# Two transformer layers on one core: where the contexts of three batches and the output biases are made

## The chip, the cores and the metric

The kernel runs on one core of a Trainium2 chip. The metric is the time on the device in microseconds (us). TensorE (PE) does matmuls, and transposes by a matmul with the identity; VectorE (DVE), ScalarE (ACT) and GpSimd (POOL) do the rest; SyncE (SP) issues most DMAs. POOL cannot read PSUM, the memory of eight banks into which TensorE writes.

## The reference

x has 4 batches of 512 rows of 256 values, 2048 rows in all (16 tiles of 128, four a batch). Two layers follow one another; each has a self-attention, a cross-attention and a feed-forward part, each with a residual and a layer norm. What matters here is layer 1:

```
x = layernorm(x + attn(x) @ Wo + bo)                 16 heads of 16, causal, rotary
x = layernorm(x + cross_attn(x, ctx_512) @ Wo + bo)   16 heads of 16, 1601 keys
x = layernorm(x + tree_ffn(x))
```

`attn` is softmax(q k / 4) v for every head. The values' bias is left out of the heads: since a softmax's weights add to one, it adds `bv @ Wo` to the output, so each attention's output bias is `bo + bv @ Wo`, computed on the chip.

## The kernel before

The kernel is a row of programs (`nc.Block`), one after another; in each, every engine has its own list of instructions in a fixed, written order, and waits on semaphores. A program ends when all engines have ended theirs. Around the change stand four:

1. `combine_and_prepare` (line 1504) adds the experts' rows to x, normalizes (the helper class `Tail`), transposes x, and projects queries, keys and values of layer 1's self-attention. VectorE begins with `val.init` (a memset), then for each chunk c of two tiles: `dve_sum`, the gathered rows' addition, `dve_stats`, and `dve_apply` of the chunk before. TensorE: `pe_proj(c)`, `pe_out(c-2)`, projections.
2. `heads_loop` with `causal` (line 1828), the first head loop: 16 groups of four heads of one batch, R = 5 buffers. Each group has four key tiles (kt) with three turns each, so 12 "points": scores of heads 0 and 1, scores of heads 2 and 3 (L2069), values (L2085) of the tile before. ScalarE takes the exponential (L2145), POOL sets the upper triangle to zero (L1981, `triangle`), and ScalarE copies a group's result to `OT` (L2135). Between the points TensorE makes "units" (L2045) for later groups, whose row maxima VectorE takes (L2191); the last group's units are made during group 13, and its shift (L2212, `shift`) is cast early in group 14. PSUM: banks 0 to 3 scores, 4 to 6 units, 7 values.
3. `heads_tail` (line 2238), the tail between the loops. It begins with the biases: VectorE spreads `bv` over columns (L2349), TensorE multiplies (L2293), VectorE adds (L2352). Then per chunk c: TensorE transposes two tiles of OT to rows by query (`by_query`, L2279); VectorE divides by the softmax's sums (`context`: L2343 reciprocal, L2345 product); TensorE turns the context (`pe_in`, L139), ScalarE copies it (L155), TensorE projects it (`pe_proj`, L166), VectorE adds x (`dve_sum`, L193) and takes statistics (L201 to L207), POOL computes rstd (L212), VectorE applies it (`dve_apply`, L219), TensorE transposes the new x (`pe_out`, L139), ScalarE copies it to xT (L256). POOL adds the output bias to x ahead of the sum (`pool_residual`, L132), and sets rows of ones in the key buffers (`ones_tile`, L1728), for which the key loads wait on SyncE. After each of the first two batches, the queries of the cross-attention are projected (L1764), split into bf16 parts (L321, L345, L325, L358) and stored (L368).
4. `heads_loop` without `causal`, the loop of the cross-attention, begins at line 2270's barrier.

VectorE's order in a step of the tail is: contexts of chunk c, apply(c-2), sum(c-1), statistics(c-1), split. TensorE's: `by_query` of chunk c, query blocks, out(c-3), projection(c-1), turn(c).

## Time and profile before

| what | us |
|---|---|
| time, median of 3 runs (lowest, highest) | 1487.79 (1482.65, 1488.82) |
| profiled execution, its own time | 1489.09 |
| its span | 1487.1 |
| the tail's window, from VectorE's first (L2349) to the next loop's first matmul (L2045) | 795.38 to 844.73 |

Line numbers (L193) are those of the kernel before. An instruction's line can be that of a helper, so L139 is both the turn of a context and the transpose of x: the names (psum<-cf_sb,t_cx or psum<-cf_sb,x_sb) tell them apart. "[0.90 <-PE psum L166]" is idle time just before the first instruction of a row and what ended it; "PEq" stands for TensorE's sequencer. PEld is the row of weight loads, which lie beside matmuls. The granted clock is a share of TensorE's 2.4 GHz: 1.00 or 0.50, with means between them.

### The profile page before, as it was taken

How to read it: one execution, taken by the hardware profiler on the slowest of the kernel's cores; microseconds unless marked ns; L12 is line 12 of the kernel's file. 1: busy time of each engine (PE TensorE's matmuls, PEld its weight loads, DVE VectorE, ACT ScalarE, POOL GpSimd, SP SyncE). 2: the span in 40 equal slices, each digit the busy share in tenths (PEclk: the TensorE clock that was granted, in tenths of full speed). 3: DMA queues.
4: the chain of work that ended last, by engine and by line, in shares of the span. 5: the costliest groups of instructions: out<-in, count | busy, mean ns of one | idle time of the engine just before them, and what ended most of it. 6: DMA issues, size and time to landing. Idle time of an engine off the chain costs nothing. (4 is left out here: it accounts for less than half of the span.)

```text
span 1487.1 us, 24888 instructions
## 1 busy us (share of the span) xinstructions
PE 1369.3 (92%) x9358; PEld 762.8 (51%) x9358; DVE 1059.4 (71%) x2351; ACT 774.8 (52%) x1067; POOL 321.7 (22%) x407
## 2 busy tenths in 40 slices
PE   6898899989999989869998889999999999999996
PEld 3565578756899886423335422333333333333285
DVE  4887466662122128968994799999999999997077
ACT  2344266631111112336763316888888888888754
POOL 3110322243000017743335440000000000000011
PEclk9999799999999999969999869999999999999999
DMA  9548533346889842674422650343222343220001
GB/s 341 194 134 246 171 122 128 122 165 226 299 279 302 272 152 79 215 222 143 131 66 60 177 164 2 85 102 80 67 67 68 86 101 80 68 67 2 1 1 57
DMA packets 152841, 198.68 MB, mean 134 GB/s; under 512 B 15723, under 2 KB 124799, under 8 KB 152594
## 3 DMA queue, kind: packets, MB, share of 16 engines
q1 hardware_dynamic: 141004, 165.34, 36.7%
q0 software_dynamic: 9200, 29.64, 6.4%
q10 hardware_dynamic: 2518, 2.13, 0.4%
q8 instruction: 74, 1.21, 0.4%
q14 instruction: 45, 0.37, 0.1%
HBM read 136.08 MB, written 60.70 MB: 132 GB/s over the span
## 5 line engine op out<-in xcount | busy, mean ns | idle before, releaser
L2194 DVE TENSOR_REDUCE xa_part<-psum 128x1 f32<-128x512 f32 (+1 forms) x768 | 462.7, 662 | 20.4 <-PE psum L2045 18.6
L2145 ACT ACTIVATE xa_P<-psum 128x1024 f32<-128x1024 f32 (+1 forms) x416 | 403.4, 1021 | 103.3 <-PE psum L2069 102.6
L2069 PE MATMUL psum<-sa_Q,xa_K 48*128 48x512 bf16 (+3 forms) x1664 | 267.0, 381 | 3.9 <-DMA sa_Q<-xa_mrow 2.9
L2045 PE MATMUL psum<-xa_K,sa_Q 48*128 48x512 bf16 (+1 forms) x768 | 239.3, 388 | 4.4 <-DVE xa_part L2194 1.5
L2085 PE MATMUL psum<-xa_P,xa_V 128*32 128x512 f32 (+1 forms) x1664 | 222.6, 607 | 0.4 <-ACT xa_P L2145 0.4
L2045 PEld LDWEIGHTS psum<-xa_K,sa_Q 48*128 48x128 bf16 x768 | 59.2, 94 | 232.5 <-DVE xa_part L2194 160.8
L2069 PEld LDWEIGHTS psum<-sa_Q,xa_K 48*128 48x128 bf16 (+3 forms) x1664 | 105.6, 97 | 68.7 <-ACT xa_P L2145 20.7
L2191 DVE CUSTOM_DVE_ANT_0 psum<-psum,cf_sb 128x512 f32<-128x512 f32 (+1 forms) x240 | 111.5, 520 | 18.3 <-PE psum L2045 17.5
L1334 PEld LDWEIGHTS psum<-xtT,wgu 128*128 128x128 f32 x992 | 115.5, 192 | 5.8 <-issue 4.6
L1334 PE MATMUL psum<-xtT,wgu 128*128 128x128 f32 x992 | 115.9, 275 | 1.4 <-issue 0.8
L2145 ACT ACTIVATE sa_P<-psum 128x1024 f32<-128x1024 f32 (+3 forms) x128 | 83.4, 702 | 49.1 <-PE psum L2069 49.1
L1483 DVE TENSOR_TENSOR ht<-sgt,psum 128x512 f32<-128x512 f32 x31 | 21.3, 688 | 114.1 <-ACT sgt L1386 114.1
L1386 ACT ACTIVATE sgt<-psum 128x512 f32<-128x512 f32 x31 | 18.5, 597 | 132.6 <-PE psum L1334 132.6
L212 POOL TENSOR_TENSOR t_rstd<-t_ve,mhalf 128x2 f32<-128x2 f32 (+1 forms) x36 | 27.6, 768 | 229.3 <-DVE t_ve L207 229.1
L2045 PE MATMUL psum<-sa_K,sa_Q 48*128 48x512 bf16 (+1 forms) x240 | 64.7, 321 | 12.1 <-PEq L1556 5.5
L2069 PE MATMUL psum<-sa_Q,sa_K 50*128 50x256 bf16 (+7 forms) x512 | 63.9, 308 | 4.0 <-DMA sa_Q<-sa_mrow 2.6
L1994 POOL CAST xa_mh<-xa_mx 128x16 bf16<-128x16 f32 x16 | 3.1, 197 | 293.0 <-DVE xa_mx L2200 266.8
L2085 PEld LDWEIGHTS psum<-xa_P,xa_V 128*32 128x32 f32 (+1 forms) x1664 | 32.9, 108 | 53.5 <-issue 50.6
L634 PE MATMUL psum<-a_in_sb,xT_sb 128*128 128x384 f32 x128 | 48.5, 526 | 12.9 <-DMA xT_sb<-in_xT 10.1
L1215 PE MATMUL psum<-xT_sb,big_weights 128*128 128x512 f32 x128 | 58.8, 614 | 0.7 <-PEq L937 0.7
L1981 POOL TENSOR_SCALAR_AFFINE_SELECT sa_P<-sa_P 128x512 f32<-128x512 f32 x64 | 40.6, 634 | 86.6 <-ACT sa_P L2145 86.6
L1344 PE MATMUL psum<-wdn,ht 128*128 128x256 f32 x248 | 58.7, 380 | 0.6 <-DVE yt L1490 0.6
(250 smaller groups left out, 2140.7 us busy)
## 6 DMA issues: line engine op xcount, KB each, us to landing
wgu<-in_f_gu SPq DMA_DIRECT2D x31, 1024.0 KB, 6.3
xa_K<-kx SPq DMA_DIRECT2D x192, 100.1 KB, 4.9
wdn<-in_f_dn SPq DMA_DIRECT2D x31, 512.0 KB, 6.5
vx<-xv_v SPq DMA_DIRECT2D x48, 256.0 KB, 3.3
xa_V<-vx POOLq DMA_DIRECT2D x16, 768.0 KB, 6.5
sa_Q<-qs SPq DMA_DIRECT2D x64, 96.0 KB, 2.3
sa_K<-ks SPq DMA_DIRECT2D x64, 96.0 KB, 2.3
sa_Q<-qx SPq DMA_DIRECT2D x64, 96.0 KB, 2.3
```

Source lines behind the costliest of these rows:

```text
L212: pool.tensor_tensor(self.rstd[:, u, :], self.ve[:, u, :], self.env.mhalf[:, 0:self.tc], ALU.pow).then_inc(self.s_rstd, 1)
L634: pe.matmul(o, env.xT[:, k, t * P:(t + 1) * P], w["a0_in"][:, k, cols], start=(k == 0), stop=False)
L1215: last = pe.matmul(o, w[name][:, k, f * P:(f + 1) * P], env.xT[:, k, c * L:(c + 1) * L], start=(k == 0), stop=(k == KD - 1))
L1334: last = pe.matmul(GU(j)[:, f * P:(f + 1) * P], wgu[:, u, k, f * P:(f + 1) * P], xtT[:, u, k, :], start=(k == 0), stop=(k == KD - 1))
L1344: last = pe.matmul(Y_PS[:, 0:D], ht[:, u, f, :], wdn[:, u, f, :], start=(f == 0), stop=(f == FC - 1))
L1981: pool.affine_select(square, square, [[0, G], [1, P]], ALU.is_ge, 0.0, base=0, channel_multiplier=-1).then_inc(s_tri, 1)
L2045: last = pe.matmul(out[:, 0:width], hb.q(u)[tile:tile + HALF, to, qt * P:(qt + 1) * P], hb.k(u)[tile:tile + HALF, to, cut[e]:cut[e] + widt ...
L2069: last = pe.matmul(out(j), hb.k(u)[tile:tile + depth, to, kt * P:kt * P + r], hb.q(u)[tile:tile + depth, to, q0(kt):L], start=(half == 0), ...
L2085: last = pe.matmul(O_PS[h * VW:(h + 1) * VW, q0(kt):L], Vg[0:r, u, kt, h * VW:(h + 1) * VW], Pr[0:r, (u * KT + kt) % PR, h, 0:L - q0(kt)], ...
L2145: act.activation(Pr[0:r, (u * KT + kt) % PR, h:h + 2, 0:w_], S_PS(p)[0:r, :, 0:w_], ACT.Exp, scale=SCALE).then_inc(s_exp, 1)
L2191: dve.tensor_tensor_reduce(src[:, 0:k1], src[:, 0:k1], env.later[:, L - k1:L], 1.0, -3e38, ALU.add, ALU.max, mx[:, g % 2, col + qt:col + q ...
L2194: dve.tensor_reduce(part[:, g % 2, col + qt, e:e + 1], src[:, 0:cut[e + 1] - cut[e]], AX, ALU.max).then_inc(s_1free, 1)
```

## The change

The class `OutputBias` takes the bias computation out of the tail and puts it into the combining program: VectorE's two spreading copies ahead of `val.init`, TensorE's eight-matmul product ahead of its first step, VectorE's two additions at the start of step 1, and a wait of TensorE (`pe_free`) before its first projection.

The class `Contexts` holds what makes contexts. During the last 21 points of the first loop (from point 3 of group 14), TensorE makes those of batches 0 to 2, twelve tiles, as `pe_ahead(t)`: `by_query(t)` into banks 4 and 5, and after every second tile the turn of chunk t/2 - 1 into bank 6. VectorE makes the contexts behind its last shift and copies the turned ones into `xT` (no longer needed there), which takes the place of `t3_cT`. At the end of its list in that loop POOL adds the bias to x for chunks 0 and 1. Context and sum buffers lie in columns of `cf` with tables no longer read.

In the tail `pe_proj(0)` comes first. Contexts of tiles 12 to 15 are made in steps 0 and 1, and turned at the head of steps 1 and 2. VectorE's order becomes apply(c-1), sum(c), statistics(c), contexts, split; POOL's residual(c+1), rstd(c), ones, split. `pe_out(c-2)` waits until all turned contexts are copied. The number of steps goes from 11 to 10.

```diff
-        self.r = sb(name + "_r", [P, ring, tc, D], F32)
+        self.r = sb(name + "_r", [P, ring, tc, D], F32) if sums is None else sums
...
+        bias_ = OutputBias(env, c_, sem)
...
@@ -1579,6 +1580,7 @@
             @block.tensor
             def _(pe):
                 pe.sem_inc(tail.s_proj, DONE)
+                bias_.pe_product(pe)
                 for c in range(STEPS):
                     if DONE <= c < CHUNKS:
                         tail.pe_proj(pe, c, lambda k: w["f_wd"][:, k, :],
@@ -1587,6 +1589,8 @@
                         tail.pe_out(pe, c - 2)
                     for n in blocks_at(c):
                         b, name, m = blocks[n]
+                        if n == 0:
+                            bias_.pe_free(pe)
                         if m == 0:
                             pe.wait_ge(tail.s_xT, TB // 2 * (b + 1))
                             item_free(pe, item_of(n))
 
             @block.vector
             def _(dve):
+                bias_.dve_spread(dve)
                 val.init(dve)
                 for c in range(STEPS):
+                    if c == 1:
+                        bias_.dve_add(dve)
                     if c < CHUNKS:
                         u = c % tail.ring
                         tail.dve_sum(dve, c, biased=False)
...
+class OutputBias:
+    def __init__(self, env, c, sem):
+        self.env = env
+        sb, _ = env.alloc(c)
+        self.bvb = sb("bvb", [P, 2, KD, P], F32)
...
+    def ps(self, n):
+        return self.env.PS[:, 7 * BANK + n * D:7 * BANK + (n + 1) * D]
+    def dve_spread(self, dve):
+        for n, of in enumerate("sx"):
+            dve.tensor_copy(self.bvb[:, n, :, :], self.env.w[of + "_bv"].unsqueeze(2).to_broadcast([P, KD, P])).then_inc(self.s_bvb, 1)
+    def pe_product(self, pe):
+        for n, of in enumerate("sx"):
+            pe.wait_ge(self.s_bvb, n + 1)
+            for k in range(KD):
+                last = pe.matmul(self.ps(n), self.bvb[:, n, k, :], self.env.w[of + "_wo"][:, k, :], start=(k == 0), stop=(k == KD - 1))
+            last.then_inc(self.s_bps, 1)
+    def dve_add(self, dve):
+        dve.wait_ge(self.s_bps, 2)
+        for n, of in enumerate("sx"):
+            dve.tensor_tensor(self.env.w[of + "_bo"], self.ps(n), self.env.w[of + "_bo"], ALU.add).then_inc(self.s_bias, 1)
+    def pe_free(self, pe):
+        pe.wait_ge(self.s_bias, 2)
+class Contexts:
+    AHEAD = (B - 1) * TB
+    STEPS = AHEAD + 1
+    def __init__(self, env, c, name, OT):
+        self.env, self.OT = env, OT
+        sb, sem = env.alloc(c)
+        spare = env.cf[:, CF_FIRST:CF].rearrange("p (a u t n) -> p a u t n", a=2, u=2, t=2)
+        self.cx = spare[:, 0]
+        self.tail = Tail(env, c, name, (2, 4, 2), PAIR_TILES, KD, behind=3, inputs=False, sums=spare[:, 1])
+        self.rc = sb(name + "_rc", [P, 2, H], F32)
...
+    def bank(self, t):
+        n = t % 2 + (4 if t < self.AHEAD else 0)
+        return self.env.PS[:, n * BANK:(n + 1) * BANK]
+    def turned(self, c):
+        return self.env.PS[:, 6 * BANK:7 * BANK] if 2 * c < self.AHEAD else self.tail.ps(0, c)
+    def columns(self, c, i, k):
+        return self.env.xT[:, k, (2 * c + i) * P:(2 * c + i + 1) * P]
+    def pe_by_query(self, pe, t):
+        b, i = divmod(t, TB)
+        if t >= 2:
+            pe.wait_ge(self.s_cx, t - 1)
+        for g in range(G):
+            last = pe.transpose(self.bank(t)[:, g * P:(g + 1) * P], self.OT[:, b * G + g, i * P:(i + 1) * P], self.env.ident)
+        last.then_inc(self.s_ops, 1)
+    def pe_in(self, pe, c):
+        if 2 * c < self.AHEAD and c:
+            pe.wait_ge(self.tail.s_cT, c)
+        elif c:
+            pe.wait_ge(self.tail.s_cT, c - 1)
+        pe.wait_ge(self.s_cx, 2 * c + 2)
+        for i in range(2):
+            last = self.tail.turn(pe, self.turned(c), i, self.cx[:, c % 2, i, :])
+        last.then_inc(self.tail.s_cT_ps, 1)
+    def pe_ahead(self, pe, t):
+        if t < self.AHEAD:
+            self.pe_by_query(pe, t)
+        if t >= 2 and t % 2 == 0:
+            self.pe_in(pe, t // 2 - 1)
+    def dve_context(self, dve, t):
+        if t >= 4:
+            dve.wait_ge(self.tail.s_cT_ps, t // 2 - 1)
+        o = self.bank(t).rearrange("p (h n) -> p h n", n=VW)
+        dve.wait_ge(self.s_ops, t + 1)
+        dve.reciprocal(self.rc[:, t % 2, :], o[:, :, HD:HD + 1].rearrange("p h n -> p (h n)")).then_inc(self.s_rc, 1)
+        dve.wait_ge(self.s_rc, t + 1)
+        dve.tensor_tensor(self.cx[:, t // 2 % 2, t % 2, :].rearrange("p (h d) -> p h d", d=HD), o[:, :, 0:HD],
+                          self.rc[:, t % 2, :].unsqueeze(2).to_broadcast([P, H, HD]), ALU.mult).then_inc(self.s_cx, 1)
+    def dve_ahead(self, dve, t):
+        if t < self.AHEAD:
+            self.dve_context(dve, t)
+        if t >= 2 and t % 2 == 0:
+            c = t // 2 - 1
+            dve.wait_ge(self.tail.s_cT_ps, c + 1)
+            dve.tensor_copy(self.env.xT[:, :, 2 * c * P:(2 * c + 2) * P],
+                            self.turned(c).rearrange("p (k n) -> p k n", k=KD)).then_inc(self.tail.s_cT, 1)
...
+    def pe_proj(self, pe, c, w):
+        pe.wait_ge(self.tail.s_cT, c + 1)
+        self.tail.pe_proj(pe, c, w, lambda i, k: self.columns(c, i, k))
...
@@ -1857,6 +1978,13 @@
     assert BEHIND < LEAD and EARLY >= LEAD
+
+    AHEAD_FROM, AHEAD_POINTS = (GROUPS - 2) * POINTS + 3, 20
+
+    def due_ahead(g, point):
+
+        past = g * POINTS + point - AHEAD_FROM
+        return min(contexts.STEPS, past * contexts.STEPS // AHEAD_POINTS + 1) if contexts and past >= 0 else 0
     def due(point, count):
@@ -2017,6 +2145,8 @@
                         triangle(g, kt)
                         if kt == 1 and 1 <= g <= GROUPS - R:
                             reload_v(g - 1, (g - 1) % R)
+                for c in range(2):
+                    contexts.tail.pool_residual(pool, c, lambda t: env.w["s_bo"])
             @block.tensor
             def _(pe):
@@ -2112,6 +2242,10 @@
                                     shift(g + 1)
                             if ahead == 1 and point == LAST_POINT:
                                 shift(g + 1)
+                            for t in range(due_ahead(g, point - 1) if point else due_ahead(g - 1, POINTS - 1), due_ahead(g, point)):
+                                if t == 0:
+                                    pe.wait_ge(s_1free, reduced(shift_at(GROUPS - 1)))
+                                contexts.pe_ahead(pe, t)
                 for n in range(U):
                     if not causal and n in project_at:
@@ -2231,158 +2365,115 @@
                     high(GROUPS - 1)
                     low(GROUPS - 1)
                     shift(GROUPS - 1)
+                    for t in range(contexts.STEPS):
+                        contexts.dve_ahead(dve, t)
                 else:
                     of_cuts(GROUPS - 1)
...
+    tail = contexts.tail
+    LAST = contexts.AHEAD // 2
+    STEPS = CHUNKS + 2
...
             @block.tensor
             def _(pe):
...
                 def query_block(n):
                     if n >= 2:
                         sp_.freed(pe, n - 2)
-                    else:
-                        pe.wait_ge(s_bias, 2)
                     later.project(pe, n, Q_PS(n))
...
                 for c in range(STEPS):
-                    if c < CHUNKS:
-                        for t in PAIR_TILES(c):
-                            by_query(t)
+                    if LAST <= c + LAST - 1 < CHUNKS:
+                        contexts.pe_in(pe, c + LAST - 1)
                     for n in blocks_at(c):
                         query_block(n)
-                    if 3 <= c < CHUNKS + 3:
-                        pe.wait_ge(tail.s_cT, min(c, CHUNKS))
-                        tail.pe_out(pe, c - 3)
-                    if 1 <= c <= CHUNKS:
-                        tail.pe_proj(pe, c - 1, lambda k: wo[:, k, :])
+                    if 2 <= c < CHUNKS + 2:
+                        pe.wait_ge(tail.s_cT, CHUNKS)
+                        tail.pe_out(pe, c - 2)
                     if c < CHUNKS:
-                        tail.pe_in(pe, c, lambda i: cx[:, (2 * c + i) % 4, :], lambda i: pe.wait_ge(s_cx, 2 * c + i + 1))
+                        contexts.pe_proj(pe, c, lambda k: wo[:, k, :])
+                    if c + LAST < CHUNKS:
+                        for t in PAIR_TILES(c + LAST):
+                            contexts.pe_by_query(pe, t)
             @block.scalar
             def _(act):
                 for c in range(STEPS):
+                    if LAST <= c + LAST - 1 < CHUNKS:
+                        contexts.act_in(act, c + LAST - 1)
                     for n in blocks_at(c):
                         sp_.act_hi(act, n, Q_PS(n))
-                    if 3 <= c < CHUNKS + 3:
-                        tail.act_out(act, c - 3)
-                    if c < CHUNKS:
-                        tail.act_in(act, c)
+                    if 2 <= c < CHUNKS + 2:
+                        tail.act_out(act, c - 2)
                     for n in blocks_at(c):
                         sp_.act_mid(act, n)
             @block.gpsimd
             def _(pool):
-                pool.wait_ge(s_bias, 1)
                 for c in range(STEPS):
+                    if 2 <= c + 1 < CHUNKS:
+                        tail.pool_residual(pool, c + 1, lambda t: bo)
                     if c < CHUNKS:
-                        tail.pool_residual(pool, c, lambda t: bo)
-                    if queries and c < 2 * hb.RING:
-                        pool.wait_ge(tail.s_xb, c + 1)
+                        tail.pool_rstd(pool, c)
+                    if c < 2 * hb.RING:
+                        pool.wait_ge(tail.s_rstd, c + 1)
                         hb.ones_tile(pool, c // 2, c % 2).then_inc(s_ones, 1)
                         pool.wait_ge(s_ones, c + 1)
-                    if 1 <= c <= CHUNKS:
-                        tail.pool_rstd(pool, c - 1)
                     for n in blocks_at(c):
                         sp_.pool_lo(pool, n)
             @block.vector
             def _(dve):
...
                 for c in range(STEPS):
+                    if 1 <= c <= CHUNKS:
+                        tail.dve_apply(dve, c - 1)
                     if c < CHUNKS:
-                        for t in PAIR_TILES(c):
-                            context(t)
-                    if 2 <= c < CHUNKS + 2:
-                        tail.dve_apply(dve, c - 2)
-                    if 1 <= c <= CHUNKS:
-                        tail.dve_sum(dve, c - 1)
-                        tail.dve_stats(dve, c - 1)
+                        tail.dve_sum(dve, c)
+                        tail.dve_stats(dve, c)
+                    if c + LAST < CHUNKS:
+                        for t in PAIR_TILES(c + LAST):
+                            contexts.dve_context(dve, t)
                     for n in blocks_at(c):
                         sp_.dve_rest(dve, n, Q_PS(n))
...
@@ -2736,11 +2827,12 @@
         with ExitStack() as c1:
             sb1, _ = alloc(c1)
             OT = sb1("OT", [P, GROUPS, L], F32)
-            heads_loop(nc, env, "sa", sa, OT, keys=later_keys)
+            contexts = Contexts(env, c1, "t3", OT)
+            heads_loop(nc, env, "sa", sa, OT, keys=later_keys, contexts=contexts)
             with ExitStack() as c2:
                 xa = HeadBuffers(env, c2, "xa", CTX, False, stacks(env.qx), kx_part, env.vx, Q=sa.Q)
-                later = heads_tail(nc, env, "t3", OT, "s", "x", xa)
+                later = heads_tail(nc, env, contexts, "s", xa)
                 heads_loop(nc, env, "xa", xa, OT, queries=later)
             l1_out(nc, env, OT, env.w["x_wo"])
```

## Rows read from the trace of the kernel before

**Rows 1.** The page, part 1: busy time, share of the span, instructions.

```profile
PE 1369.3 (92%) x9358; PEld 762.8 (51%) x9358; DVE 1059.4 (71%) x2351; ACT 774.8 (52%) x1067; POOL 321.7 (22%) x407
```

**Rows 2.** Windows, first head loop: busy us of PE, PEld, DVE, ACT, POOL; clock; DMA.

```profile
764.50:772.70 8.20, 7.57 (x82) 3.26 (x81) 7.73 (x37) 5.43 (x10) 2.54 (x4) 1.00 0.02 4
...
781.00:794.00 13.00, 9.96 (x116) 3.05 (x116) 0.00 (x0) 9.34 (x17) 5.08 (x8) 1.00 0.01 2
```

**Rows 3.** Timeline, loop's end: start, duration (us), engine, line, operation, [idle before].

```profile
780.18 0.28 DVE L2212 CAST sa_mrow<-psum 32x128 bf16<-32x128 f32 x1 [0.40 <-PE psum L2054]
...
793.07 0.64 POOL L1981 TENSOR_SCALAR_AFFINE_SELECT sa_P<-sa_P 128x512 f32<-128x512 f32 x1 [0.42 <-ACT sa_P L2145]
...
793.76 0.42 PE L2085 MATMUL psum<-sa_P,sa_V 128*32 128x128 f32 x8 [0.42 <-POOL sa_P L1981]
...
794.25 0.60 ACT L2135 ACTIVATE OT<-psum 128x512 f32<-128x512 f32 x1 [1.25 <-PE psum L2085]
...
795.38 0.29 DVE L2349 COPY t_bvb<-s_bv_sb 128x256 f32<-128x256 f32 x1 [14.92 <-PEq L1917]
```

**Rows 4.** Timeline, the tail's first steps and the next loop's first matmul.

```profile
797.21 1.91 PE L2293 MATMUL psum<-x_wo_sb,t_bvb 128*128 128x256 f32 x4
...
799.16 0.42 DVE L2352 TENSOR_TENSOR s_bo_sb<-psum,s_bo_sb 128x256 f32<-128x256 f32 x1 [3.28 <-PE psum L2293]
...
799.67 1.41 POOL L132 TENSOR_TENSOR x_sb<-x_sb,s_bo_sb 128x256 f32<-128x256 f32 x2 [5.96 <-DVE s_bo_sb L2352]
...
802.43 1.97 PE L166 MATMUL psum<-s_wo_sb,t_cT 128*128 128x256 f32 x8
...
804.56 0.90 PEld L2279 LDWEIGHTS psum<-cf_sb,OT 128*128 128x128 f32 x8
...
844.73 0.96 PE L2045 MATMUL psum<-xa_K,sa_Q 48*128 48x512 bf16 x3 [1.00 <-PEq L2270]
```

**Rows 5.** Timeline, VectorE and POOL in the tail.

```profile
804.44 0.69 DVE L193 TENSOR_TENSOR t_r<-psum,x_sb 128x512 f32<-128x512 f32 x1 [0.90 <-PE psum L166]
...
806.23 0.17 DVE L207 TENSOR_SCALAR t_ve<-t_mv 128x2 f32<-128x2 f32 x1
806.31 0.26 DVE L2343 RECIPROCAL t_rc<-psum 128x16 f32<-128x16 f32 x1
...
808.78 0.68 DVE L193 TENSOR_TENSOR t_r<-psum,x_sb 128x512 f32<-128x512 f32 x1
...
811.90 1.27 DVE L219 TENSOR_SCALAR x_sb<-t_r,t_mv,t_rstd 128x256 f32<-128x256 f32 x2
813.09 0.68 DVE L193 TENSOR_TENSOR t_r<-psum,x_sb 128x512 f32<-128x512 f32 x1
...
823.30 0.69 DVE L193 TENSOR_TENSOR t_r<-psum,x_sb 128x512 f32<-128x512 f32 x1 [1.52 <-PE psum L166]
...
839.50 0.68 DVE L193 TENSOR_TENSOR t_r<-psum,x_sb 128x512 f32<-128x512 f32 x1
...
841.53 0.69 POOL L212 TENSOR_TENSOR t_rstd<-t_ve,mhalf 128x2 f32<-128x2 f32 x1 [0.94 <-DVE t_ve L207]
...
842.26 0.74 DVE L219 TENSOR_SCALAR x_sb<-t_r,t_mv,t_rstd 128x256 f32<-128x256 f32 x2 [0.80 <-POOL t_rstd L212]
```

**Rows 6.** Windows around both boundaries; the clock stands third from the end.

```profile
796.00:800.00 4.00, 4.00 (x15) 3.24 (x15) 0.84 (x3) 0.00 (x0) 0.33 (x1) 0.57 0.01 2
...
848.00:852.00 4.00, 4.00 (x8) 1.11 (x6) 2.51 (x4) 0.69 (x1) 0.00 (x0) 0.50 0.59 159
```

**Rows 7.** Timeline of the combining program's start.

```profile
560.27 5.57 PE L166 MATMUL psum<-big_weights,hT 128*128 128x256 f32 x16 [6.18 <-DVE t_r L193]
...
564.77 0.73 DVE L219 TENSOR_SCALAR x_sb<-t_r,t_mv,t_rstd 128x256 f32<-128x256 f32 x2
565.68 0.60 PE L139 MATMUL psum<-cf_sb,x_sb 128*128 128x128 f32 x4
```

**Rows 8.** Window of the combining program's middle.

```profile
580.00:600.00 20.00, 20.00 (x83) 14.40 (x82) 17.01 (x31) 6.32 (x12) 12.95 (x11) 1.00 0.19 64
```

More of the change, by code:

```diff
@@ L82, with __init__ @@
 class Tail:
-    def __init__(self, env, c, name, banks, tiles, kc, behind=0, inputs=True, copied=False, slots=None, scaled=False):
+    def __init__(self, env, c, name, banks, tiles, kc, behind=0, inputs=True, copied=False, slots=None, scaled=False, sums=None):
         self.env, self.tiles, self.kc, self.banks, self.behind = env, tiles, kc, banks, behind
@@ L2385, in heads_tail, with _, keys @@
-    return later if queries else None
+            @block.sync
+            def _(sp):
+                def keys(g):
+                    sp.wait_ge(s_ones, 2 * g + 2)
+                    hb.load_k(sp, g, g)
+                keys(0)
+                for dst, src in env.loads["d"]:
+                    sp.dma_start(dst, src).then_inc(s_wd, 16)
+                keys(1)
+                for n in range(KD):
+                    sp_.sp_out(sp, n)
+                sp_.sp_end(sp, KD)
+                hb.load_q(sp, 0, 0)
+                for n in range(KD, 2 * KD):
+                    sp_.sp_out(sp, n)
+                sp.wait_ge(s_wd, 16 * len(env.loads["d"]))
@@ L2389, in l1_out @@
+    return later
 def l1_out(nc, env, OT, wo):
```

86 lines of the change are left out of this document (19 added, 67 removed).

## The prediction

> **What bounds the kernel now.** I read part 1 of the page first: TensorE is busy 92% of the span, but that is an average over a dozen stages [rows 1]. The change touches three stretches, so I read each by itself.
>
> The first is the last two groups of the first head loop. The per-window view shows VectorE stop at 780.46 us (its last cast); then it does nothing, while a window of 8.2 us before had it busy for 7.73 [rows 2, 3]. TensorE shows 9.96 us busy in 13, so 3.04 us free [rows 2]. The order is a chain: scores, exponential on ScalarE, triangle on POOL, values. After the last triangle (ends 793.71) come the last values (794.18) and the copy to OT (794.85); then the program ends on all engines together, since VectorE, long done, is released only at 795.38, "<-PEq L1917" [rows 3].
>
> The second is the tail, 795.4 to 844.7. Chunk 0 reaches its sum (L193) at 804.44, chunk 7 at 839.50, and the next loop's first matmul stands at 844.73 [rows 4, 5]. In an ordinary chunk VectorE is the busy one: sum at 804.44, variance at 806.23, two contexts from 806.31 to 807.57, apply, next sum at 808.78, 4.34 us with no idle time. Before the sum at 823.30 it waits 1.52 us for TensorE, which had query projections ahead [rows 5].
>
> The third is the start of the combining program: TensorE busy from 560.27 with `pe_proj`, VectorE's apply from 564.77 to 565.50, and TensorE's transpose behind both at 565.68 [rows 7].
>
> **The change, part by part.**
>
> *Contexts in the loop.* Four transposes for each of twelve tiles and each of six chunks: 72 on TensorE. Eight took 0.90 us of weight-load row, 0.112 each [rows 4], so 8.1 us are added within points 3 of group 14 to 10 of group 15. VectorE's share (12 x 0.64, from two contexts in 1.26 us, and six copies of about the 0.68 us of L193) is 12 us, hidden in its 14 us idle [rows 2, 5]; it cannot start before the cast at 780.46. TensorE is not idle enough: 8.1 - 3.04 = 5.1 us longer if all idle time is filled. Laying the steps into the order by hand (each transpose group behind its scores or values, values behind the triangle, and the last turn behind context 11, 0.5 us) I get 5.6. Bounds: 8.1 if nothing hides; and 0 if the matmuls' ends overstate, since the weight-load row is busy only 3.05 us of the 13 [rows 2]. I take 5.6, nearer to the busy row.
>
> Here the Trainium skill ("Perfetto Trace Analysis", "Identifying the Most-Contended Engine") speaks for the change: it says that matmul busy share is not a good measure of TensorE's closeness to its limit, and asks for the weight-load share instead. By that 77% of the window is free and the growth is near 0; it feeds the second rival below. Against it stands that a group still has its chain of waits.
>
> *Two residuals on POOL at the loop's end.* `pool_residual` of chunks 0 and 1 stands behind the last triangle in POOL's order: four additions, two in 1.41 us [rows 4], so 2.9 us after 793.71. The copy to OT ends 1.14 us after it. As all engines leave together, the end moves by 1.75 us, whatever the growth. In the tail the same additions lay beside other work. Bounds: 0 (if POOL did not have to be waited for) and 2.9.
>
> *The tail's start.* From 794.85 to the first sum now 9.59 us pass: bias copies, products, additions, two tiles' contexts, the turn, the copy, the projection. After: 0.6 us to leave and enter, then `pe_proj(0)` at once. At full clock it takes 1.97 us [rows 4]. But the granted clock was 0.57 in the window 796 to 800, after TensorE had been idle from 794.18 to 795.73, and four 256-column matmuls then took 1.91 us with the last one's end [rows 3, 4, 6]. With POOL's residuals the idle time is 3 us, so I count eight at that pace: 3.6. So 4.2 us instead of 9.59, 5.4 saved; 7.0 at full clock. First sum: 804.44 + 5.6 + 1.75 - 5.4 = 806.4.
>
> *Sum 0 to sum 7, now 35.06 us* [rows 5]. Chunks 2 to 7 lose their contexts; chunks 6 and 7's are made in steps 0 and 1. But TensorE's order in steps 1 and 2 is turn(6), projection(1) and turn(7), transposes out(0), projection(2), and turn(c) waits for contexts that VectorE makes after its statistics. Sum 0 to the end of two contexts is 3.2 us, then turn and projection 2.5: 5.75 instead of 4.34. In step 2 out(0) waits also for ScalarE's copy (`wait_ge(tail.s_cT, CHUNKS)`), so contexts 3.2, turn 0.5, copy 0.7, out 0.5, projection 1.9 and a handover: 7.0 instead of 4.31. That loses 4.1. The five later intervals are 26.4 us now. They lose 6.3 of contexts on VectorE's row, but behind them appears what they hid: statistics to rstd 0.25, rstd 0.69, then apply 0.74, so an undisturbed interval is 1.78 + 0.25 + 0.69 + 0.04 + 0.74 = 3.5 [rows 5]. And four of the five hold query projections (3.6 us of TensorE before the chunk's own), their split on VectorE (1.3) or POOL's residual ahead of rstd. Walked through: 3.8, 4.5, 4.9, 5.6, 4.7 = 23.5, a gain of 2.9. Sum: 36.3, 1.2 longer. Bounds: 35.06 - 6 x 1.26 = 27.5, and 41 (third rival).
>
> Apply depends on what POOL does: 1.27 us for two while POOL added residuals, 0.74 with POOL idle [rows 5]. POOL's memsets of the key rows (1.43) now follow rstd and lie on apply, and no row has that overlap; 0.74 to 1.27 per chunk, and I take 1.2 in the first six.
>
> The Trainium skill ("GPSIMD Engine Reference", "Key points") says that GpSimd shares its SBUF interfaces with VectorE and contends with instructions in a 2-port mode or with two inputs. Apply's rows agree (1.27 against 0.74); whether a memset contends too no row here shows.
>
> *SyncE.* The key loads wait for the memsets, which follow rstd: keys(0) goes out some 5 us later, keys(1) to about 834. Stores of the first queries then queue for a microsecond or two; the query load still lands before the end. I cost it at nothing; with more delay it would be next.
>
> End of tail: 806.4 + 36.3 + 5.2 (sum 7 to the next loop, unchanged) = 847.9 against 844.73: +3.2.
>
> *Biases in the combining program.* VectorE gets two copies ahead of its memset (0.29 each at 0.21 distance, 0.45) and two additions ahead of sum 1 (0.42 each at 0.34 distance, 0.76) [rows 3, 4]. Apply(0) then ends 1.2 later, at 566.7, against TensorE's transpose at 565.68: TensorE, which then has no idle time (20.00 of 20 us) [rows 8], starts 1.0 later. The products themselves lie in its idle time before 560.27 [rows 7]. +1.0; bounds 0 and 1.2. A warmer clock for `pe_proj(2)` (5.57 us, 3.62 is usual) gives nothing, since apply(0) is then last.
>
> Sum: +3.2 + 1.0 = +4.2 us. The profiled run took 1489.09 (span 1487.1), 1.3 over the median 1487.79; I apply the difference to the median: 1492.
>
> **Rivals.**
>
> 1. Forecast: transposes lengthen the loop, POOL's residuals and the order in steps 1 and 2 eat what the shorter start gives. +1 to +7, 1489 to 1495. Chance 0.5.
>
> 2. Faster: VectorE's row decides the tail. Then six chunks lose 1.26 us each: 35.06 to 27.5, the end at 806.4 + 27.5 + 5.2 = 839.1, -5.6, and with +1.0 the time is 1483. If TensorE also hides half the growth (-2.8) 1480. For it: no idle time on VectorE in the ordinary chunks. Against: TensorE's order behind the contexts, and VectorE's wait for TensorE at 823.30 already [rows 5]. It decides if turn(6) and turn(7) cost projection(1) and (2) nothing. Chance 0.25, half of it beyond 0.5%.
>
> 3. Slower: the clock. TensorE idles 3 us at the boundary and then works in pieces; at 848 to 852, four us after the next loop's start, the clock still stood at 0.50 though the row was full [rows 6]. If it stays at 1.2 GHz through step 2, projections 1 and 2 cost 1.6 more each and three groups of transposes 0.45 each: +4.6, 1497; with the loop's transposes unhidden (+2.5) 1499. It decides if the granted clock in the tail's first 12 us is under 0.7. Chance 0.25, nearly all beyond 0.5%.
>
> **Numbers.** A median can tell about 0.5% (7.4 us) from no change: below 1480.4, above 1495.2. Faster 0.13 (half of rival 2), slower 0.25 (rival 3 and the forecast's edge), same 0.62. Range 1481 to 1498: rival 2 without its best end, rival 3 without its worst. The forecast's own range is 1489 to 1495.
>
> **What would show it.** Loop: the last OT copy at about 800.5, triangles no longer followed at once by values. Boundary: POOL's L132 as the last before the barrier, some 1.7 us behind the OT copy. Tail: sum 0 at 806 to 807; intervals of 5.7 and 7 before sums 1 and 2 with VectorE waiting for projection; then 3.8 to 5.6. Combining: every stage from 566 on 1 us later. I am wrong if the loop's end moves by under 2 us, if steps 1 and 2 take 4.3, or if the clock stays down.

## The result, and the profile after

The changed kernel takes 1498.7 us (median; lowest 1494.72), the kernel before 1486.99 beside it: ratio 1.0079, 95% interval 1.0060 to 1.0098. It is slower by 11.7 us; I had forecast 4.2, and 1498 as the upper end. One run of this kernel (3370 us) and one of e10 (1911 us) fell into a slow state: their medians count them (1497.5 and 1495.9 without), their ratios do not. The profiled execution took 1502.37 us (span 1500.4). A second series of the same kernel (e11, below) gave 1.0089 [1.0070, 1.0109], 14.3 us.

Part 1 of the page says little, as before [rows 1]:

```profile
PE 1376.4 (92%) x9358; PEld 767.8 (51%) x9358; DVE 1069.4 (71%) x2357; ACT 770.8 (51%) x1061; POOL 320.9 (21%) x407
```

So I cut both traces at the same events. "Combining" runs from the last copy of the feed-forward part (L1490 after) to the loop's first matmul, "loop's end" from group 13's copy to OT to the last one, "start" from that copy's end to sum 0 (L193).

| stretch, us | before | forecast | after | e11 |
|---|---|---|---|---|
| combining | 99.05 | +1.0 | 101.04 | 101.06 |
| loop up to group 13's copy | 134.74 | 0 | 133.74 | 134.73 |
| loop's end | 13.24 | +5.6 | 19.98 | 19.97 |
| start | 9.59 | -3.65 | 6.36 | 6.52 |
| sum 0 to sum 7 | 35.06 | +1.2 | 42.84 | 41.37 |
| sum 7 to the next loop | 5.23 | 0 | 5.69 | 5.68 |

(The forecast's -3.65 is 1.75 for the residuals less 5.4 for the start.) e11's stretches add up to 12.4 us more than before, 8.3 above the forecast: 5.1 of them in sum 0 to sum 7, 1.1 at the loop's end, 1.0 in combining, 0.6 at the start, 0.5 at the end. The line that failed is sum 0 to sum 7. Its seven intervals, for the kernels that the argument needs:

| us | 1 | 2 | 3 | 4 | 5 | 6 | 7 |
|---|---|---|---|---|---|---|---|
| before | 4.34 | 4.31 | 4.29 | 5.92 | 6.44 | 5.08 | 4.68 |
| forecast | 5.75 | 7.0 | 3.8 | 4.5 | 4.9 | 5.6 | 4.7 |
| after | 7.30 | 9.55 | 5.10 | 5.09 | 5.51 | 5.63 | 4.66 |
| e11, the same kernel | 7.20 | 7.10 | 5.10 | 5.09 | 5.53 | 6.66 | 4.69 |
| e2, residuals in the tail | 5.76 | 9.62 | 5.10 | 5.09 | 5.52 | 5.63 | 4.67 |
| e9, fillers on TensorE | 5.76 | 7.09 | 5.10 | 5.09 | 5.52 | 5.63 | 4.67 |
| e3, memsets moved | 7.25 | 7.11 | 4.30 | 4.24 | 4.24 | 6.25 | 4.68 |
| e5, projection first | 5.13 | 5.10 | 5.08 | 5.09 | 5.51 | 6.70 | 4.68 |
| e8, one batch ahead | 4.65 | 4.31 | 4.31 | 5.76 | 6.98 | 4.78 | 4.68 |

Timeline after, TensorE at the boundary and in steps 1 and 2 (columns as in [rows 3]):

```profile
800.99 0.86 PE L2215 MATMUL psum<-sa_P,sa_V 128*32 128x256 f32 x16
805.57 3.27 PE L166 MATMUL psum<-s_wo_sb,xT_sb 128*128 128x256 f32 x8 [3.72 <-PEq L2045]
808.63 1.45 PE L1868 MATMUL psum<-cf_sb,OT 128*128 128x128 f32 x8
812.24 0.63 PE L139 MATMUL psum<-cf_sb 128*128 128x128 f32 x4 [2.15 <-DVE cf_sb L1894]
812.71 3.44 PE L166 MATMUL psum<-s_wo_sb,xT_sb 128*128 128x256 f32 x8
815.93 1.22 PE L1868 MATMUL psum<-cf_sb,OT 128*128 128x128 f32 x8
819.54 0.94 PE L139 MATMUL psum<-cf_sb 128*128 128x128 f32 x4 [2.38 <-DVE cf_sb L1894]
821.16 1.12 PE L139 MATMUL psum<-cf_sb,x_sb 128*128 128x128 f32 x4 [0.69 <-ACT xT_sb L1908]
822.07 3.62 PE L166 MATMUL psum<-s_wo_sb,xT_sb 128*128 128x256 f32 x8
```

The order in steps 1 and 2 is as forecast: projections 1 and 2 stand behind a turn that waits for VectorE's contexts (2.15, 2.38 us), step 2 also for ScalarE's copy (0.69). Projection 0 takes 3.27 us, near the 3.6 forecast; but projections 1 and 2 take 3.44 and 3.62, where I had counted 1.9. The windows (columns as in [rows 2]) show TensorE in pieces and at a low clock:

```profile
804.00:808.00 4.00, 2.43 (x7) 2.05 (x8) 0.00 (x0) 0.00 (x0) 0.00 (x0) 0.76 0.00 2
808.00:812.00 4.00, 2.09 (x10) 1.57 (x9) 2.95 (x10) 0.00 (x0) 1.01 (x2) 0.82 0.00 0
812.00:816.00 4.00, 3.76 (x13) 3.01 (x14) 2.08 (x3) 0.60 (x1) 2.57 (x3) 0.61 0.00 0
...
820.00:824.00 4.00, 3.31 (x12) 2.56 (x11) 1.37 (x2) 1.25 (x3) 1.87 (x3) 0.50 0.34 85
```

VectorE and POOL after, around sums 1 to 3:

```profile
812.01 2.06 DVE L219 TENSOR_SCALAR x_sb<-cf_sb,t_mv,t_rstd 128x256 f32<-128x256 f32 x2
816.18 0.69 DVE L193 TENSOR_TENSOR cf_sb<-psum,x_sb 128x512 f32<-128x512 f32 x1 [2.10 <-PE psum L166]
...
825.73 0.69 DVE L193 TENSOR_TENSOR cf_sb<-psum,x_sb 128x512 f32<-128x512 f32 x1 [4.37 <-PE psum L166]
...
828.51 2.40 DVE L219 TENSOR_SCALAR x_sb<-cf_sb,t_mv,t_rstd 128x256 f32<-128x256 f32 x2 [0.81 <-POOL t_rstd L212]
830.83 0.68 DVE L193 TENSOR_TENSOR cf_sb<-psum,x_sb 128x512 f32<-128x512 f32 x1
```

```profile
827.78 0.69 POOL L212 TENSOR_TENSOR t_rstd<-t_ve,mhalf 128x2 f32<-128x2 f32 x1 [5.83 <-DVE t_ve L207]
828.53 1.42 POOL L1735 MEMSET xa_K<- 32x1601 f32 x1
830.04 1.46 POOL L132 TENSOR_TENSOR x_sb<-x_sb,s_bo_sb 128x256 f32<-128x256 f32 x2
```

Apply starts at 828.51, the memset at 828.53: 2.40 us for the pair, against 1.27 beside residual additions and 0.74 with POOL idle [rows 5].

### The profile page after: what moved, and what is told of

It is laid out like the page before. It is cut to its first block and busy times, and to the rows that moved or that the text cites. A ratio compares the mean times of both kernels' runs of the same rounds, so it can differ in the third digit from the quotient of the medians.

```text
span 1500.4 us, 24878 instructions
## 1 busy us (share of the span) xinstructions
PE 1376.4 (92%) x9358; PEld 767.8 (51%) x9358; DVE 1069.4 (71%) x2357; ACT 770.8 (51%) x1061; POOL 320.9 (21%) x407
## 5 line engine op out<-in xcount | busy, mean ns | idle before, releaser
L2215 PEld LDWEIGHTS psum<-xa_P,xa_V 128*32 128x32 f32 (+1 forms) x1664 | 33.0, 108 | 53.6 <-issue 50.3
```

The lines of the kernel that those rows point to most:

```text
L2215: last = pe.matmul(O_PS[h * VW:(h + 1) * VW, q0(kt):L], Vg[0:r, u, kt, h * VW:(h + 1) * VW], Pr[0:r, (u * KT + kt) % PR, h, 0:L - q0(kt)], ...
```

## The experiments

All ratios are to the kernel before on the same chip, with 95% intervals. Stages that an edit does not touch differ by 1 to 3 us between two profiles (the rest of the span after the tail was 639.6 to 643.0 us in all), so an edit is judged by its own stretch, and the median says what is left of it. "Tail" is the time from the last copy to OT to the next loop's first matmul: 49.88 us before, 54.89 in the changed kernel's first profile, 53.57 in e11's.

**e1, the bias part alone** (the kernel before, with `OutputBias` and nothing of `Contexts`):

```diff
 (kernel before, heads_tail)
-                dve.wait_ge(s_bps, 2)
-                for n, of in enumerate((here, later_)):
-                    dve.tensor_tensor(w[of + "_bo"], B_PS(n), w[of + "_bo"], ALU.add).then_inc(s_bias, 1)
...
 (combine_and_prepare)
+                    if c == 1:
+                        bias_.dve_add(dve)
```

> The kernel before with the biases alone moved to the combining program; the tail keeps its contexts. Theory (each part has its own price, and the contexts' part carries the loss): the first sum comes some 4 us earlier after the loop's end (9.59 us to about 5.5), the combining program ends about 1.0 us later, so 2 to 4 us faster than before, about 1484. Rival (the biases' move carries part of the loss): the combining program loses 3 us or more and the time is not under before's.

Measured: 1486.55 against 1487.11, ratio 1.0004 [0.9990, 1.0018]. The start went from 9.59 to 6.86 us (I had expected about 5.5), sum 0 to sum 7 stayed at 35.06. Combining grew by 0.36. So the start is 2.7 us shorter in this profile; the 2 to 4 us that I expected in the median are not there.

**e2, the residuals of chunks 0 and 1 back in the tail:**

```diff
 (POOL, end of the first loop)
-                for c in range(2):
-                    contexts.tail.pool_residual(pool, c, lambda t: env.w["s_bo"])
 (POOL, start of the tail)
+                for c in range(2):
+                    tail.pool_residual(pool, c, lambda t: bo)
```

> The changed kernel with POOL's residuals of chunks 0 and 1 taken out of the first loop's list and put at the head of POOL's list in the tail. Theory (they hold the loop's end, and a program that POOL ends last is left 1 us later still): TensorE's first matmul of the tail comes at most 1 us after the last OT copy instead of 3.1, and the time falls by 2 to 3 us from the changed kernel's. Rival (the barrier costs the same whoever is last; only 1.4 us of POOL's work goes): 1.4 us, and 1.6 us still pass from the last instruction to the first.

Measured: 1496.96, ratio 1.0064 [1.0043, 1.0086]; the start fell from 6.36 to 2.31 us. Its timeline, POOL, ScalarE and TensorE:

```profile
801.42 0.64 POOL L2109 TENSOR_SCALAR_AFFINE_SELECT sa_P<-sa_P 128x512 f32<-128x512 f32 x1 [1.80 <-ACT sa_P L2277]
803.72 2.79 POOL L132 TENSOR_TENSOR x_sb<-x_sb,s_bo_sb 128x256 f32<-128x256 f32 x4 [1.67 <-POOLq L2045]
```

```profile
802.83 0.60 ACT L2267 ACTIVATE OT<-psum 128x512 f32<-128x512 f32 x1 [1.47 <-PE psum L2213]
```

```profile
803.73 1.97 PE L166 MATMUL psum<-s_wo_sb,xT_sb 128*128 128x256 f32 x8 [0.97 <-PEq L2045]
```

The next program starts 0.30 us after ScalarE's end (803.43) and 1.67 after POOL's (802.06). In the changed kernel it starts 3.05 after ScalarE's end and again 1.67 after POOL's (801.12 + 2.78 = 803.90; 805.57). So the residuals cost their whole length. Projection 0, after 0.97 us of idle instead of 3.72, ran at full clock here; the short idle time alone does not secure that, since in e6, after the same 0.97, it took 3.63 (below). With projection 1 at full clock too, interval 1 is 5.76; interval 2 is 9.62, as in the first profile, with projection 2 at the low clock.

```profile
801.12 2.78 POOL L132 TENSOR_TENSOR x_sb<-x_sb,s_bo_sb 128x256 f32<-128x256 f32 x4
```

**e3, POOL's memsets away from apply** (three in front of rstd(0), two and one behind the residuals of steps 0 and 1):

```diff
...
+                early = {0: (3, 4), 1: (5,)}
...
+                for n in range(3):
+                    ones(n)
                 for c in range(STEPS):
-                    if 2 <= c + 1 < CHUNKS:
-                        tail.pool_residual(pool, c + 1, lambda t: bo)
                     if c < CHUNKS:
                         tail.pool_rstd(pool, c)
-                    if c < 2 * hb.RING:
-                        pool.wait_ge(tail.s_rstd, c + 1)
-                        hb.ones_tile(pool, c // 2, c % 2).then_inc(s_ones, 1)
-                        pool.wait_ge(s_ones, c + 1)
+                    if 2 <= c + 2 < CHUNKS:
+                        tail.pool_residual(pool, c + 2, lambda t: bo)
+                        if c in early:
+                            pool.wait_ge(tail.s_xb, c + 3)
+                    for n in early.get(c, ()):
+                        ones(n)
```

> The changed kernel with POOL's memsets of the key rows taken from behind rstd: three at the tail's head, two in step 0, one in step 1. Theory (a memset on POOL holds back VectorE's apply, 2.40 us a pair beside it against 0.74 alone): from chunk 2 on apply falls to 0.75 to 1.3 us, and the tail is 4 to 6 us shorter. Rival (apply is slow by the residual addition behind it, or by its new buffer in cf): apply stays at 2 us or more.

Measured: intervals 3 to 5 are 4.30, 4.24, 4.24 instead of 5.10, 5.09, 5.51 (-2.9 us); apply, with a residual beside it:

```profile
828.67 1.54 DVE L219 TENSOR_SCALAR x_sb<-cf_sb,t_mv,t_rstd 128x256 f32<-128x256 f32 x2 [0.88 <-POOL t_rstd L212]
830.14 0.68 DVE L193 TENSOR_TENSOR cf_sb<-psum,x_sb 128x512 f32<-128x512 f32 x1
...
832.91 1.54 DVE L219 TENSOR_SCALAR x_sb<-cf_sb,t_mv,t_rstd 128x256 f32<-128x256 f32 x2 [0.81 <-POOL t_rstd L212]
```

The edit moved the residual too, to a place beside apply, and apply is shorter all the same: the memset is the cause of its 2.40 us. The median, 1497.84, ratio 1.0076 [1.0054, 1.0099], does not show the gain.

**e4 and e9, TensorE kept busy** by matmuls of no use: e4 with twelve behind the loop's last values and eight in steps 0 and 1, e9 with six and three.

```diff
                 values(GROUPS - 1, (GROUPS - 1) % R, KT - 1, None)
+                if contexts:
+                    for n in range(12):
+                        pe.matmul(PS[:, 4 * BANK:4 * BANK + D], env.ident, env.w["s_wo"][:, n % KD, :], start=True, stop=True)
 (tail, behind the transposes of steps 0 and 1)
+                        for n in range(8):
+                            pe.matmul(PS[:, 7 * BANK:7 * BANK + D], env.ident, wo[:, n % KD, :], start=True, stop=True)
```

> The changed kernel with idle matmuls of TensorE whose result nobody reads: 12 behind the last values of the first loop, 8 after the transposes of steps 0 and 1. Theory (the low clock in the tail's first 20 us costs 4 to 5 us): the granted clock stays over 0.9 from 804 to 828, projection 0 to 2 take 1.9 us instead of 3.3 to 3.6, and the sums 0 to 2 come 4 us earlier. Rival (VectorE's contexts and not TensorE's pace set sums 1 and 2): the clock is kept and the sums stay within 1 us of the changed kernel's, or fillers delay the turns and the time grows.

> The changed kernel with TensorE kept busy by fewer fillers than in e4_clock_kept: six 256-column matmuls of no use behind the loop's last values (they took 0.44 us each there, so 2.6 us beside the 3.7 us in which TensorE waits at the boundary), and three behind the transposes of steps 0 and 1. Theory (the low clock costs the first two intervals 2 to 4 us, and e4 gave it back by fillers that stood in the way): projections 1 and 2 at under 2.2 us, sum 0 to sum 7 at 39 to 41 us, tail at 50 to 52 instead of 54.9, median 3 to 5 us under the changed kernel's, 1494 to 1496. Rival (the clock is a companion, the interval is set by the waits for contexts): clock 1.00 but sum 0 to sum 7 still above 41.5, median 1497 to 1500.

Measured, e4: 1499.58, 1.0087 [1.0067, 1.0107]. Each filler took 0.45 us, 3.6 for eight, and they delayed what stood behind them: the start is 7.01, intervals 1 and 2 are 6.49 and 7.84 (tail 53.02), although the projections are back at 1.9. e9: 1498.53, 1.0075 [1.0062, 1.0089]. Its clock is 1.00 in every window of 4 us from 796 to 832, and intervals 1 and 2 are 5.76 and 7.09, where I had worked out 5.75 and 7.0. TensorE in e9's steps 0 to 2:

```profile
807.22 1.97 PE L166 MATMUL psum<-s_wo_sb,xT_sb 128*128 128x256 f32 x8 [0.94 <-PEq L2045]
809.02 1.04 PE L1868 MATMUL psum<-cf_sb,OT 128*128 128x128 f32 x8
809.89 1.46 PE L2421 MATMUL psum<-s_wo_sb,cf_sb 128*128 128x256 f32 x6
812.58 0.63 PE L139 MATMUL psum<-cf_sb 128*128 128x128 f32 x4 [1.23 <-DVE cf_sb L1894]
813.04 1.89 PE L166 MATMUL psum<-s_wo_sb,xT_sb 128*128 128x256 f32 x8
...
820.14 1.89 PE L166 MATMUL psum<-s_wo_sb,xT_sb 128*128 128x256 f32 x8
```

So the excess in those two intervals is the low clock. (e2's interval 1 of 5.76, without fillers, says the same.) The tail is 49.60 us, 5.3 shorter than in the first profile of the changed kernel and 4.0 than in e11's; the median is not lower. I can't place that: in e9's profile the loop up to group 13 took 135.91 and the rest after the tail 642.74 us, 1.2 and 2.8 more than in e11's, and medians can't say which of these is typical.

**e5, projection ahead of the turn in steps 0 to 2:**

```diff
                 for c in range(STEPS):
+                    if c <= 2:
+                        contexts.pe_proj(pe, c, lambda k: wo[:, k, :])
                     if LAST <= c + LAST - 1 < CHUNKS:
                         contexts.pe_in(pe, c + LAST - 1)
...
-                    if c < CHUNKS:
+                    if 2 < c < CHUNKS:
                         contexts.pe_proj(pe, c, lambda k: wo[:, k, :])
```

> The changed kernel with projection(c) ahead of turn(c+5) in TensorE's steps 1 and 2. Theory (projections 1 and 2 are late because they stand behind turns that wait for VectorE's contexts): sum 1 comes 5 us or less after sum 0 (7.3 in the changed kernel) and sum 2 some 5 us after sum 1 (9.55); the tail is 4 to 6 us shorter. Rival (the low clock is what makes them late): TensorE stays at half clock and the tail is at most 2 us shorter.

Measured: 1494.3, ratio 1.0050 [1.0031, 1.0069]; the median is 4.4 us under the changed kernel's, on another chip and with overlapping intervals of the ratio. Intervals 1 and 2 are 5.13 and 5.10, set by VectorE's row, although projection 0 met the low clock (tail 49.81).

```profile
806.83 3.75 PE L166 MATMUL psum<-s_wo_sb,xT_sb 128*128 128x256 f32 x8 [3.71 <-PEq L2045]
810.37 1.73 PE L1868 MATMUL psum<-cf_sb,OT 128*128 128x128 f32 x8
811.94 1.89 PE L166 MATMUL psum<-s_wo_sb,xT_sb 128*128 128x256 f32 x8
813.98 0.64 PE L139 MATMUL psum<-cf_sb 128*128 128x128 f32 x4
```

**e6 and e10, e2, e3 and e5 together**, in e10 also with fillers (four at the loop's end, three in steps 0 and 1, two in steps 2 to 7):

```diff
...
 (e10, TensorE, behind the transposes; e6 has none of it)
+                        for n in range(3):
+                            pe.matmul(PS[:, 7 * BANK:7 * BANK + D], env.ident, wo[:, n % KD, :], start=True, stop=True)
+                    elif c < CHUNKS:
+                        for n in range(2):
+                            pe.matmul(PS[:, 0:D], env.ident, wo[:, n % KD, :], start=True, stop=True)
```

> The changed kernel with the residuals in the tail, the memsets early and the projections first, all three. Theory (each has its own price): from the last OT copy to the next loop's first matmul it takes 42 to 45 us against 54.9 in the changed kernel and 49.9 before, and the time comes to about before's, 1485 to 1489, since the loop's 6.7 us and the combining program's 1 stay. Rival (the repairs share one cause, the clock): 48 us or more, 1493 or more.

> e6_three_repairs with fillers for TensorE: four behind the loop's last values, three in steps 0 and 1, two in each step from 2 to 7. In e6 the clock fell to 0.50 to 0.64 in three stretches, and projections took 3.63 and 3.57 us, a query projection 5.26. Theory (the clock is what ate the three repairs): projections 1.9 us, query projections 3.6, intervals 4.3 to 5, sum 0 to sum 7 at 34 to 36 instead of 39.5, tail at 43 to 46 instead of 49.2, median 1488 to 1490. Rival (the engines' order and VectorE's row hold it, a full clock changes little, and sixteen fillers of 0.2 to 0.4 us cost some of it): tail at 48 to 50, median 1492 to 1495.

Measured, e6: 1493.46, 1.0054 [1.0032, 1.0075], tail 49.19 us, no shorter than with one repair alone (49.4 to 50.3, that is 4.5 to 5.5 from 54.89 and 3.2 to 4.2 from e11's). e10: 1496.38, 1.0060 [1.0045, 1.0074], tail 49.23, with a clock of 1.00 from 796 to 840 but for 0.66 and 0.91 in two windows. So a full clock with fillers in the way does not shorten e6; what it would give without them stays open. What holds e10 back stands in its VectorE row: waits for POOL, where three memsets stood ahead of rstd(0), and for projections, where fillers and query projections stood ahead. e6's row has waits for the same two (1.16, 0.87 and 0.81 for POOL; 1.64, 1.28 and 3.25 for projections), and its first projection met the low clock.

```profile
800.65 3.63 PE L166 MATMUL psum<-s_wo_sb,xT_sb 128*128 128x256 f32 x8 [0.97 <-PEq L2045]
```

(This row is e6's, the next ones are e10's.)

```profile
810.53 1.55 DVE L219 TENSOR_SCALAR x_sb<-cf_sb,t_mv,t_rstd 128x256 f32<-128x256 f32 x2 [2.66 <-POOL t_rstd L212]
...
822.80 0.69 DVE L193 TENSOR_TENSOR cf_sb<-psum,x_sb 128x512 f32<-128x512 f32 x1 [1.12 <-PE psum L166]
...
829.27 0.69 DVE L193 TENSOR_TENSOR cf_sb<-psum,x_sb 128x512 f32<-128x512 f32 x1 [2.14 <-PE psum L166]
```

```profile
805.30 4.39 POOL L1735 MEMSET xa_K<- 32x1601 f32 x3
809.78 0.71 POOL L212 TENSOR_TENSOR t_rstd<-t_ve,mhalf 128x2 f32<-128x2 f32 x1
```

**e7, the loop's 48 transposes to rows by query made twice:**

```diff
-        for g in range(G):
+        for g in range(G) if t >= self.AHEAD else [*range(G)] * 2:
             last = pe.transpose(self.bank(t)[:, g * P:(g + 1) * P], ...
```

> The changed kernel with the 48 transposes of OT in the loop's last groups issued twice, VectorE's and ScalarE's work as it is. Theory (TensorE is full there and every transpose lengthens the loop): from the OT copy of group 13 to the last one it takes 25 to 27 us, against 20.0 in the changed kernel and 13.2 before. Rival (waits for contexts and for VectorE are what lengthens it): 20 to 22 us.

Measured: 1502.92, ratio 1.0117 [1.0087, 1.0146]; the loop's end grew from 19.98 to 24.76, 4.78 / 48 = 0.10 us a transpose. Each further transpose lengthens the loop. TensorE's matmul row is full there, though its weight-load row is not (windows of the changed kernel, then of e7):

```profile
787.00:800.00 13.00, 12.80 (x124) 7.35 (x123) 8.29 (x23) 5.90 (x10) 2.54 (x4) 1.00 0.00 0
```

```profile
787.00:800.00 13.00, 13.00 (x126) 8.93 (x125) 6.56 (x17) 5.23 (x9) 1.90 (x3) 1.00 0.01 1
```

**e8, only one batch's contexts in the loop**, the rest in the tail one chunk after another, with the residuals in the tail, the projection ahead of the turn, POOL's memsets behind the residuals instead of behind rstd, and the bias part kept:

```diff
-    AHEAD = (B - 1) * TB
+    AHEAD = TB
...
 (TensorE's step: turn last)
...
-                        pe.wait_ge(tail.s_cT, CHUNKS)
+                        pe.wait_ge(tail.s_cT, min(c + 1, CHUNKS))
                         tail.pe_out(pe, c - 2)
...
+                    if LAST <= c + LAST - 1 < CHUNKS:
+                        contexts.pe_in(pe, c + LAST - 1)
...
```

> The changed kernel with one batch's contexts (4 tiles) in the loop instead of three, residuals in the tail, contexts of chunk c+2 made in step c with projection first, the memsets between residuals as before. Theory: the loop is only 2 to 2.5 us longer than before's (24 transposes instead of 72), the first sum comes 3 us after the last OT copy instead of 9.6, chunks take 4.3 us: the time is 1482 to 1485, faster than both kernels. Rival (a tail that starts at once only meets the low clock, and its order costs as much): within 2 us of before's.

Measured: 1484.02 against 1487.23, ratio 0.9975 [0.9964, 0.9986]: faster than both kernels, by 0.25% against the one before. The loop's end grows by 1.36 us for 24 transposes, the start is 2.53, sum 0 to sum 7 35.47, the tail 43.67 instead of 49.88 us; combining takes 2.0 of it back. Against e6, which moves three batches with much the same order, the loop's end is 5.4 us shorter and the tail 5.5. VectorE has no idle time in an ordinary chunk: rstd is ready behind the contexts.

```profile
808.81 0.25 DVE L1894 RECIPROCAL t_rc<-psum 128x16 f32<-128x16 f32 x1
809.09 0.43 DVE L1896 TENSOR_TENSOR cf_sb<-psum,t_rc 128x256 f32<-128x256 f32 x1
809.43 1.27 DVE L219 TENSOR_SCALAR x_sb<-cf_sb,t_mv,t_rstd 128x256 f32<-128x256 f32 x2
810.62 0.68 DVE L193 TENSOR_TENSOR cf_sb<-psum,x_sb 128x512 f32<-128x512 f32 x1
```

**e11, the changed kernel again:**

> The changed kernel as it is, for a second profiled execution and more times. The profiled execution of the changed kernel took 1502.4 us, above the kernel's median of 1498.7, and e9's tail was 5.3 us shorter in its profile while its median was the same. If the low clock in steps 1 and 2 is there in every execution: sum 0 to sum 7 again at 42 to 43, tail at 54 to 55, with projections of 3.4 to 3.6 us. If it is a matter of the single execution: projections 1 and 2 partly at 1.9 to 2.2, tail at 50 to 53, and the profiled execution at 1497 to 1500. Either way the median stays at 1497 to 1500, and the loop's growth (the 19.98 us from group 13's copy to the last) and the gap of 1.67 us behind the last residual stay as they were.

Measured: 1499.59 against 1485.29, 1.0089 [1.0070, 1.0109]. Interval 1 is 7.20 again, interval 2 is 7.10 instead of 9.55 (projection 2 at 1.89 us): the 2.45 us in interval 2 are there in some executions (the first, and e2's with 9.62) and not in others (e11, e3, e7: 7.10 or 7.11). In interval 6 e11 lost 1.0 us in which VectorE waited for a projection: the query projection ahead of it took 5.37 us instead of 3.67, in a window with a clock of 0.68.

## Why the prediction was wrong

1. **Sum 0 to sum 7: the step that failed**, forecast +1.2, measured +7.8 (e11: +6.3). The order of TensorE in steps 1 and 2 was read rightly: e9, at full clock, has its two intervals within 0.1 us of the forecast. Two prices were missing. The clock: I took it at full after projection 0, it fell again, and intervals 1 and 2 were 4.1 us longer than worked out (e11: 1.55). I had that as rival 3, with a chance of 0.25 and the same price of 1.6 us a projection; its condition (under 0.7 in the first 12 us) was too strict, the windows show 0.76, 0.82 and 0.61. And the memsets: I took apply beside one at up to 1.27 us, because no row had the overlap; it takes 2.05 to 2.42. Intervals 3 to 7 are 26.0 instead of 23.5; e3, without the overlap, has 23.7 (in sum: its intervals 5 and 6 are 0.7 under and over the forecast). 4.1 + 2.5 is the whole excess of 6.6 in the first profile; e11's 5.1 is 1.55 plus 2.5 plus 1.0 in interval 6, which is the low clock again.

   That 1.27 was no upper bound stood in the trace of before: one pair of applies there took 2.08 us, beside POOL's split (L358). The memsets had harmed nothing, since they lay beside sums: 0.68 us each, as with POOL idle (0.69 at 816.18 after).

```profile
813.08 1.46 POOL L1728 MEMSET xa_K<- 32x1601 f32 x1
...
826.65 2.27 POOL L358 TENSOR_TENSOR xq_parts<-xq_rest,xq_parts 128x512 bf16<-128x512 f32 x2 [0.55 <-ACT xq_parts L325]
827.74 2.08 DVE L219 TENSOR_SCALAR x_sb<-t_r,t_mv,t_rstd 128x256 f32<-128x256 f32 x2
```

   (Rows of the kernel before; the sum beside the memset, at 813.09, is in [rows 5].)

2. **The residuals at the loop's end.** I let the program end with whichever engine ended last and counted 1.75 us. The trace of before already had the distance: the last triangle ends at 793.71 and VectorE is released at 795.38, 1.67 later, while ScalarE's 794.85 [rows 3] is only 0.53 before. With the same 1.67 in the later profiles, POOL decided there too, so a longer POOL moves the start by all of its 2.78. From the OT copy's end to sum 0 I had 5.95 us and it took 6.36: 3.05 to the next program's first matmul where I had 2.35, and 3.31 for the projection where I had 3.6.

3. **The loop's growth**, 5.6 forecast, 6.74 measured, is inside its bounds. Only 8.1 - 6.7 = 1.4 us of transposes found TensorE idle, an estimate at my price of 0.112 us each (at e7's 0.10 it is 0.5), where my walk through the order had 2.5. The rule that I had weighed (the Trainium skill, "Perfetto Trace Analysis", "Identifying the Most-Contended Engine": matmul busy share is not a good measure, go by the weight-load share) would have said no growth at 3.05 of 13 us [rows 2]. e7 disagrees: with that row at 7.35 of 13 in the changed kernel, each further transpose cost 0.10 us. In this stretch of f32 matmuls the matmul row was the measure.

4. **Combining.** +1.0 was right up to 77 us into it, where all of VectorE's events are 1.0 later. Then the key projection (usual price 3.60) took 6.68 instead of 5.54 us, both partly at a low clock, and the stretch ended 2.0 later. It did so, by 1.9 to 2.2, in ten of the twelve profiles with the biases moved (the key projection at 6.14 to 6.74); in e1 and e10 it ended 0.4 later, with a key projection of 5.07. That a shift of 1 us changes how much of a low-clock stretch an instruction catches is my reading; no run tests it. In the first profile the loop behind it took 1.0 less; e11's did not.

```profile
628.58 5.54 PE L1594 MATMUL psum<-xT_sb,s_wk_sb 128*128 128x512 f32 x8
```

```profile
629.36 6.68 PE L1598 MATMUL psum<-xT_sb,s_wk_sb 128*128 128x512 f32 x8
```

(The first row is of the kernel before, the second of the changed one.)

5. **Sum 7 to the next loop** cost +0.46, forecast 0. It is the clock once more: the last transposes took 1.09 us (855.32, window 852 to 856 at 0.73), and 0.63 before (843.10).

6. **Rival 2** asked whether VectorE's row decides. In e5 it does, and a chunk without contexts still takes 5.08 (interval 3), where before one with contexts took 4.3. VectorE now waits for POOL's rstd (0.81), which the contexts had covered, and applies beside the memset. Without that overlap (e3) a chunk takes 4.24 to 4.30, as long as interval 3 of before with two contexts in it: there the 1.26 us taken out of the row bring nothing. Where VectorE's split (1.40 us) stands ahead of apply it covers rstd, and e3's five later intervals together take 23.7 us where the kernel before took 26.4.

What stays open: why e9's shorter tail does not show in its median, and whether the same holds for e3. Not tried: contexts one batch ahead with the biases in the tail, which would spare the combining program's 2 us and give up the biases' part of the shorter start (2.7 us in e1).

## What to carry to other kernels

Before work is moved off a busy row, ask what that work covered: here the contexts hid rstd's latency. And ask what a new order puts side by side: the memset moved behind rstd met apply, with contexts ahead of it or not. Moving a quarter of the contexts, in a better order (e8), made the kernel faster; moving three quarters made it slower, with much the same order too (e6, 1.0054). At a program's boundary look for each engine's own distance between its last instruction and the next start; the latest sum of end and distance sets it, and what is appended to that engine costs its full length. A reordering that leaves TensorE in pieces has to be priced at both levels of the clock.
